# A mixture-of-experts block on one core: the first five expert tiles formed in the last steps of the mixer stage, and the early sums' pieces gathered in each group's first step

## The reference, cut to what matters

```python
h = _layernorm(x) * (1 + ca) + sa
x = x + ga * mixer(h)                    # silu(h @ Win + b), a decaying scan over time, @ Wout
h = _layernorm(x) * (1 + cb) + sb
logits = h @ Wr + br                     # 8 experts, each token goes to its best two
u = layernorm(relu(h @ W1[e] + b1[e]))   # 128 -> 512
y = layernorm(relu(u @ W2[e] + b2[e]))   # 512 -> 128
x = x + gb * (gate0 * y[e0] + gate1 * y[e1])
```

## Time and profile before

| | us |
|---|---|
| median of three runs | 512.86 |
| the profiled execution's own time | 515.06 |
| its span, first to last instruction | 513.1 |
| PE busy | 487.1 (95%) |
| DVE busy | 445.1 (87%) |
| ACT busy | 412.6 (80%) |
| POOL busy | 360.1 (70%) |

### The profile page before, as it was taken

The page is one execution under the profiler, slowest core; times in us unless marked ns, Lnnn a source line. Parts: engine busy times, 40 slices in busy tenths (PEclk is TensorE's granted clock), DMA queues, the critical chain, the costliest instruction groups (busy, mean ns, idle before and its releaser), DMA issues. The chain is left out here.

```text
span 513.1 us, 15015 instructions
## 1 busy us (share of the span) xinstructions
PE 487.1 (95%) x3051; PEld 372.0 (72%) x3051; DVE 445.1 (87%) x2217; ACT 412.6 (80%) x1140; POOL 360.1 (70%) x483
## 2 busy tenths in 40 slices
PE   7989999999987799999999999999999999999994
PEld 6445656555545588888888778888888888888861
DVE  7779999998887599888887789999999999999994
ACT  3679887978764588889888888898888898999984
POOL 1003666666667778888888878788787788988871
PEclk9999999999995699999999999999999999999998
DMA  6980111154111568878726686765766667666665
GB/s 167 309 240 21 46 48 46 48 130 114 52 47 55 135 151 164 161 225 198 178 89 157 178 204 162 191 194 159 208 190 145 192 208 203 175 180 207 189 177 164
DMA packets 80329, 78.36 MB, mean 153 GB/s; under 512 B 11420, under 2 KB 73015, under 8 KB 80242
## 3 DMA queue, kind: packets, MB, share of 16 engines
q1 hardware_dynamic: 71826, 60.48, 46.9%
q0 software_dynamic: 8416, 16.93, 9.3%
HBM read 55.20 MB, written 22.62 MB: 152 GB/s over the span
## 5 line engine op out<-in xcount | busy, mean ns | idle before, releaser
L683 POOL DMA_INDIRECT expert_rows<-rows_ring,slot x128 | 123.3, 964 | 94.5 <-issue 78.4
L711 POOL DMA_INDIRECT expert_results<-y,target x119 | 120.8, 1015 | 30.6 <-issue 24.5
L1725 PE MATMUL bank<-W,h2T 128*128 x720 | 97.4, 278 | 1.8 <-issue 0.8
L1725 PEld LDWEIGHTS bank<-W,h2T 128*128 128x128 f32 x720 | 88.2, 193 | 13.1 <-issue 6.7
L906 ACT ACTIVATE v<-wmod 128x128 f32<-128x128 f32 x135 | 41.8, 310 | 40.0 <-DVE vg L1409 35.0
L1612 PE MATMUL bank<-W1hi,h3hi 128*128 x135 | 66.6, 494 | 1.4 <-DVE h3lo L1176 1.4
L792 ACT ACTIVATE n<-X,nm,rs 128x128 f32<-128x128 f32 x128 | 54.1, 485 | 12.8 <-DVE nm L1343 12.8
L1398 DVE SCALAR_TENSOR_TENSOR wmod<-bank,rse,shifts 128x128 f32<-128x128 f32 x119 | 41.0, 344 | 24.2 <-PE bank L1725 23.3
L1181 DVE BATCH_NORM_STATS2 stf<-h1T 128x6 f32<-128x512 f32 x90 | 59.3, 659 | 0.4 <-ACT h1T L803 0.4
L1620 PE MATMUL bank<-ident_wr,h1T 128*128 128x128 f32 x360 | 55.2, 276 | 0.0
L1613 PE MATMUL bank<-W1lo,h3hi 128*128 x135 | 54.4, 403 | 0.0
(11 more groups left out here) (249 smaller groups left out, 1196.9 us busy)
## 6 DMA issues: line engine op xcount, KB each, us to landing
shifts<-expert_shifts SPq DMA_DIRECT2D x119, 192.0 KB
hrow<-expert_rows SPq DMA_DIRECT2D x135, 65.0 KB
xi<-expert_results SPq DMA_DIRECT2D x12, 512.0 KB, 5.2
out_x<-X SPq DMA_DIRECT2D x15, 256.0 KB
X<-in_L_attn_x SPq DMA_DIRECT2D x7, 512.0 KB, 7.4
b_ring<-b_two_parts SPq DMA_DIRECT2D x135, 4.0 KB
W1lo<-in_L_ffn_W SPq DMA_DIRECT2D x4, 512.0 KB, 6.7
expert_rows<-rows_ring,slot POOLq DMA_INDIRECT x128
```

Of the source, the lines that this page charges most:

```text
L683: nc.gpsimd.indirect_dma_start(out=rows_d, out_offset=bass.IndirectOffsetOnAxis(ap=slot[q][:, n // TOPK, n % TOPK:n % TOPK + 1], axis=0), ...
L711: nc.gpsimd.indirect_dma_start(out=results_d, out_offset=bass.IndirectOffsetOnAxis(ap=target[i % TARGETS][:], axis=0), in_=y[k], in_offset ...
L1725: ins = mm(acc, rT[(s - 4) % DEPTH][:, ch * P:(ch + 1) * P], W2[:, bass.ds(e4 * CF + ch, 1), :], start=(ch == 0), stop=(ch == CF - 1))
```

## The change

**Tiles 0 to 4 in the first stage.** Before, tiles 0 and 1 were turned in mixer step 16 and their hidden products stood at the ends of steps 16 and 17; tile 2 and all later ones had their hidden products in `expert_step(s)`. Now the hidden products of tiles 0 and 1 stand in step 16, those of tiles 2 and 3 in step 17 and those of tile 4 in step 18, with the rounding on ACT and DVE, the turns and the first value products placed between the parts of the mixer and the routing. On DVE the low part of tile 2 now stands between the maximum and the index search of batch 14, and that of tile 4 between those of batch 15; they wait for ACT, which waits for PE's turns. The two last steps of scaling W2 move to the end of step 17. On PE 7 and 9 products of the identity with itself (`keep_busy`, into a bank that nobody reads) stand in step 16, where PE waits. `expert_step` leaves out for tiles up to 4 what was done. The last count of routed tokens goes into another bank.

**Pieces gathered.** `pieces_at(i)` now gives all pieces whose tile lies in the group that begins at i, and nothing for the other steps. On ACT they stand behind the first `hidden_turned` of the group, ahead of the relu, the scale and the root of the step (before: at the end of the step). On DVE the sums stand in the same step (before: in the next). SP's program, `piece_tile` and the places of the loads are as before.

```diff
-        first_rows = [bank[4][:, 0:P], bank[0][:, 0:P]]
+        first_rows = [bank[n][:, 0:P] for n in (4, 5, 5, 4)]
-        EARLY_H = 2
+        EARLY_H = 4
         def pieces_at(i):
-            return [(b, j) for b in range(EARLY) for j in range(J) if piece_tile(b, j) == i]
+            return [(b, j) for b in range(EARLY) for j in range(J) if piece_tile(b, j) // TOGETHER * TOGETHER == i]
...
+                if s == B + 1:
+                    high_part(2, first_rows[2])
+                    hidden(0)
+                    high_part(3, first_rows[3])
...
                 if s == B:
-                    for i in range(EARLY_H):
-                        high_part(i, first_rows[i])
+                    high_part(0, first_rows[0])
+                    high_part(1, first_rows[1])
                 if s == B + 1:
-                    hidden(0)
+                    hidden(1)
+                    hidden_turned(0)
...
             run(mixer_step, FIRST1)
-            hidden(1)
-            hidden_turned(0)
+            high_part(EARLY_H, rows_bank(EARLY_H)[:, 0:P])
+            hidden(2)
+            hidden_turned(1)
+            act.wait_ge(stf_ready, 1)
+            hidden(3)
...
-                if on(s - 3, EXPERT_TILES) and s > 3 and turned_first:
+                if on(s - 3, EXPERT_TILES) and s > 4 and turned_first:
                     hidden_turned(s - 3)
+                for b, j in pieces_at(s):
+                    early_y0g(b, j)
...
-                for b, j in pieces_at(s):
-                    early_y0g(b, j)
...
                 if s == B + 1:
-                    for i in range(EARLY_H):
-                        low_part(i, first_rows[i])
+                    low_part(0, first_rows[0])
+                    low_part(1, first_rows[1])
                 if s == B + 2:
                     hidden_stats(0)
+                    hidden_stats(1)
...
+                if s == B + 1:
+                    low_part(2, first_rows[2])
+                if s == B + 2:
+                    low_part(EARLY_H, rows_bank(EARLY_H)[:, 0:P])
...
+                if s == B + 1:
+                    low_part(3, first_rows[3])
...
+                if s == B + 1:
+                    scale_w2(B + 2, 0)
+                    scale_w2(B + 2, 1)
...
-                for b, j in pieces_at(s - 1):
+                for b, j in pieces_at(s):
                     early_sum(b, j)
...
                     load_expert(0)
+                    keep_busy(7, to=1)
...
+                if s == B + 1:
+                    hidden(2)
+                    load_expert(3)
+                if s == B + 2:
+                    pe.wait_ge(rows_ready, B)
+                    turn_rows(EARLY_H, rows_bank(EARLY_H)[:, 0:P])
+                    pe.wait_ge(w2_ready, W2_STEPS)
+                    values(0)
+                    hidden(EARLY_H)
+                    load_expert(EARLY_H + 1)
...
                 if s == B:
-                    for i in range(EARLY_H):
-                        turn_rows(i, first_rows[i])
+                    turn_rows(0, first_rows[0])
+                    pe.wait_ge(x1_ready, B)
+                    turn_rows(1, first_rows[1])
+                    keep_busy(9, to=1)
+                if s == B + 1:
+                    pe.wait_ge(h3lo_ready, EARLY_H)
+                    turn_hidden(0)
...
-                if s in (B, B + 1):
-                    hidden(s - B)
-                    load_expert(s - B + 1)
+                if s == B:
+                    hidden(0)
+                    load_expert(1)
+                    hidden(1)
+                    load_expert(2)
+                    turn_rows(2, first_rows[2])
+                    turn_rows(3, first_rows[3])
                 if s == B + 1:
-                    turn_hidden(0)
+                    hidden(3)
+                    load_expert(EARLY_H)
+                    turn_hidden(1)
...
+            pe.wait_ge(placed_ready, B)
             pe.wait_ge(carry_ready, B)
-            pe.wait_ge(x1_ready, B)
-            mm(bank[5][:, 0:E], ones[:], hots[B % 2][:, J, :], start=True, stop=True).then_inc(count_done, 1)
+            mm(bank[7][:, COUNTS], ones[:], hots[B % 2][:, J, :], start=True, stop=True).then_inc(count_done, 1)
+            turn_hidden(EARLY_H - 2)
+            pe.wait_ge(counts_ready, 1)
+            turn_rows(EARLY_H + 1, rows_bank(EARLY_H + 1)[:, 0:P])
...
-                if on(s, EXPERT_TILES) and s >= EARLY_H:
+                if on(s, EXPERT_TILES) and s > EARLY_H:
                     hidden(s)
```

More of the change, by code:

```diff
@@ L892, in expert_step @@
                 last_of_group = s % TOGETHER == 0
-                if on(s + 1, EXPERT_TILES) and s + 1 >= EARLY_H:
+                if on(s + 1, EXPERT_TILES) and s + 1 > EARLY_H:
                     high_part(s + 1, rows_bank(s + 1)[:, 0:P])
@@ L906, in expert_step @@
                     nc.scalar.activation(v[1 - q][:], v0[1 - q], ACT.Relu).then_inc(v_ready, 1)
-                if on(s - 3, EXPERT_TILES) and s > 3 and not turned_first:
+                if on(s - 3, EXPERT_TILES) and s > 4 and not turned_first:
                     hidden_turned(s - 3)
@@ L1076, in round2_table @@
                     dve.wait_ge(count_done, 1)
-                    vec.tensor_copy(cnt_i[:, GROUPS - 1, :], bank[5][:, 0:E]).then_inc(counts_ready, 1)
+                    vec.tensor_copy(cnt_i[:, GROUPS - 1, :], bank[7][:, COUNTS]).then_inc(counts_ready, 1)
                 if n == 1:
@@ L1216, in mixer_step @@
                                       ALU.add).then_inc(logit_ready, 1)
-                scale_w2(s, 0)
+                if s < B + 2:
+                    scale_w2(s, 0)
                 round1_table(s, 0)
@@ L1224, in mixer_step @@
                     ins.then_inc(best_ready, 1)
-                scale_w2(s, 1)
+                if s == B + 1:
+                    low_part(2, first_rows[2])
+                if s == B + 2:
+                    low_part(EARLY_H, rows_bank(EARLY_H)[:, 0:P])
+                if s < B + 2:
+                    scale_w2(s, 1)
                 round1_table(s, 1)
@@ L1249, in mixer_step @@
                     vec.tensor_copy(rows[k3][:, :, 1], besti[p][:, :, 0]).then_inc(ids_ready, 1)
+                if s == B + 1:
+                    low_part(3, first_rows[3])
+                if s == B + 2:
+                    dve.wait_ge(best_ready, B)
+                    vec.tensor_tensor(lead[:], best[:, :, 0], best[:, :, 1], ALU.subtract).then_inc(lead_ready, 1)
                 if on(a, B):
@@ L1372, in _ @@
             run(mixer_step, 1)
-            dve.wait_ge(best_ready, B)
-            vec.tensor_tensor(lead[:], best[:, :, 0], best[:, :, 1], ALU.subtract).then_inc(lead_ready, 1)
             dve.wait_ge(table_ready, 1)
@@ L1468, in expert_step @@
                     ins = hidden_norm(s, q, p)
-                if on(s - 2, EXPERT_TILES) and s > 2 and not stats_first:
+                if on(s - 2, EXPERT_TILES) and s > 3 and not stats_first:
                     hidden_stats(s - 2)
@@ L1507, in _ @@
             run_tiles(expert_step)
-            for i in range(EXPERT_TILES - 1, EXPERT_TILES + 2):
+            for i in range(EXPERT_TILES, EXPERT_TILES + 2):
                 for b, j in pieces_at(i):
@@ L1621, in turn_hidden, with values @@
                 ins.then_inc(tr_done, 1)
+            def values(i):
+                e = expert_of[i]
+                acc = value_bank[:, 0:D].rearrange("p (o d) -> p o d", o=1)
+                pe.wait_ge(rT_ready, i + 1)
+                if i > 0:
+                    pe.wait_ge(v0_ready, i)
+                for ch in range(CF):
+                    ins = mm(acc, rT[i % DEPTH][:, ch * P:(ch + 1) * P], W2[:, bass.ds(e * CF + ch, 1), :],
+                             start=(ch == 0), stop=(ch == CF - 1))
+                ins.then_inc(y_done, 1)
             def mixer_step(s, q, e, k):
@@ L1705, in expert_step @@
+            turn_hidden(EARLY_H - 2)
+            pe.wait_ge(counts_ready, 1)
+            turn_rows(EARLY_H + 1, rows_bank(EARLY_H + 1)[:, 0:P])
             def expert_step(s, n):
-                q = n % 2
-                if on(s, EXPERT_TILES) and s >= EARLY_H:
+                if on(s, EXPERT_TILES) and s > EARLY_H:
                     hidden(s)
-                if on(s + 2, EXPERT_TILES):
-                    if s % TOGETHER == 0 and s > 0:
+                if on(s + 2, EXPERT_TILES) and s >= EARLY_H:
+                    if s % TOGETHER == 0:
@@ L1711, in expert_step @@
                         pe.wait_ge(r_ready, s)
                     turn_rows(s + 2, rows_bank(s + 2)[:, 0:P])
-                if on(s + 1, EXPERT_TILES) and s + 1 > EARLY_H:
+                if on(s + 1, EXPERT_TILES) and s > EARLY_H:
                     load_expert(s + 1)
[L1715 to L1719, removed]
+                if on(s - 4, EXPERT_TILES) and s > EARLY_H:
+                    if s == TABLE2_STEPS:
@@ L1727, in expert_step @@
-                    ins.then_inc(y_done, 1)
```

(3 more changed lines are left out.)

10 lines of the change are left out of this document (1 added, 9 removed).

## The result

| | before | after |
|---|---|---|
| median of 6 runs each, same chip | 513.14 us (512.39 to 513.94) | 538.03 us (536.94 to 539.25) |
| ratio, 95% interval | | 1.0459 [1.0433, 1.0485] |
| span of the profiled execution | 513.1 us | 537.1 us |
| first hidden product of tile 5 / 48 / 80 / 108 | 178.83 / 279.72 / 356.98 / 424.20 | 170.98 / 280.66 / 356.84 / 448.26 |

The change makes the kernel slower by 24.9 us; I had forecast 531.6, 18.7 over the median, and a range of 519 to 539. The last row of the table tells the story. PE is 7.9 us ahead at tile 5, has nothing left of it at tile 48, is level with before at tile 80, and loses 24.2 us between tiles 80 and 108.

What follows compares the result with a forecast made beforehand. POOL's full list, through SP, was taken to hold PE from 163.5 to 301 us, PE itself to bound tiles 80 to 108; 0.6 - 2.4 + 4.6 + 10.6 + 0.4 + 4.9 = +18.7 on 512.86 gave 531.6 us, range 519 to 539.

Steps and rivals of the forecast that it cites:

- lead of the first part on the path, POOL's delay: End of first stage: PE's 7 us lead is worth nothing on the path; added DVE waits delay POOL's list, +0.6 us.
- sums no longer in odd steps, tiles 80 to 108: Tiles 80 to 108: sums in odd steps delay DVE; gathering them gives back 2.4 us (0 to 2.9).
- batch 0's piece: Step 52 instead of 53: the piece waits for its load and delays tile 54, +0.4 us (0 to 1.5).
- four waits for loads, clock held: Steps 80, 88, 96, 104: pieces of batches 4 to 7 wait for SP's loads, +4.6 and +10.6 us.
- fall of the clock in them: PE's clock drops to its lower level in two of the four load waits, +4.9 us (0 to 10).
- The bound: Up to tile 48: POOL's full list holds SP, and SP holds PE, turning tile 48's rows no earlier than 274.88.
- Rival (d): POOL's list isn't full, the 7 us lead passes: 524.6 with waits (chance 0.05), 504.5 without (0.03).
- The landing: Time from SP's issue of a load until it lands, taken as 4.2 us, lower end 3, upper 5.2.
- Rival (b): Clock falls in all four waits and at the first stage's end, POOL starting 3 us late: 539 us, chance 0.10.
- The identity products: End of first stage: 16 added products, some 0.11 us each, lie in PE's waits and cost nothing.
- The shared port: DVE and GpSimd exclude each other there; two sums in a row could be held, shrinking the 2.4 us to nothing.
- Rival (c): SP issues batch 4's load before about 353, so loads are in time: 511.5 us, faster, chance 0.09.

Runs made afterwards that it cites:

- e6: The changed kernel with 13 identity products on PE in each of the four waits for late loads: 531.86 us, 1.0346.
- e5: e3 with POOL's row stores thinned to one in every fourth tile up to tile 24: 507.28 us, 0.9876.
- e9: e5 with the pieces of batch 0 left in their own tiles: 507.89 us, 0.9889.
- e10: e1 with POOL's row stores thinned to one in every fourth tile up to tile 24: 507.46 us, 0.9886.
- e3: The changed kernel with SP's loads of batches 4 to 10 moved to the first tile of their group: 512.60 us, 0.9954.
- e1: The changed kernel with the gathered pieces put back, so the first part of the change alone: 513.04 us, 0.9971.
- e11: The changed kernel with SP's loads of batches 4 to 7 one place sooner in SP's list: 518.02 us, 1.0089.
- e12: e1 without its 16 identity products at the end of the first stage: 517.27 us, 1.0084.

## Why the prediction was right, and which terms were off

| term | forecast | found |
|---|---|---|
| lead of the first part on the path, POOL's delay | +0.6 | tile 48 +0.94, tile 60 -0.06: 0 |
| sums no longer in odd steps, tiles 80 to 108 | -2.4 | -2.7, with the four late groups at 9.19 |
| batch 0's piece | +0.4 | within the first row |
| four waits for loads, clock held | +15.2 | +19.1 (e6) |
| fall of the clock in them | +4.9 | +7.8 by the traces, 6.2 by the medians |
| sum | +18.7 | +24.2; the spans differ by 24.0 |

The path was right, and the size only because the range had room: 538.03 is 1 us from the upper end of 519 to 539, and outside the 527.5 to 537 to which I gave 0.50.

**The bound** was right in every step: POOL at 267, SP's shifts behind it, PE's wait of 4.14 us in step 45 (I said 3 to 5), tile 48's rows at 275.7 (I said 274.9; the clock fell in that wait, which I had not counted). Rival (d), that POOL's list isn't full, is out: the lead passes only where that list is thinned, in e5, e9 and e10.

**The landing was the term that was mis-sized most.** I took 4.2 us for the load, from batch 0's single piece, which gave an upper end for one load; the page's median over twelve, 5.2, stood beside it. The four took 5.06, 5.38, 6.04 and 5.06 in the changed kernel and 4.82, 6.50, 5.13 and 4.96 in e6, where the mean is 5.35: 1.15 over mine, four times, is 4.6, and the waits were off by 3.9. The rest of that sum holds: without the fall of the clock tile 82 comes at 366.07 in e6, where I had 365.8, and each group of e6 loses ACT's wait less 0.1 to 0.4 us. Two slips in my sum come to 0.5 us and change nothing: 3.5 three times is 10.5, and 6.5 us at 3.51 for 2.30 lose 2.2.

**The clock** fell with all four waits and not with two. The Trainium skill, TensorE: Matmul & The Clock Gate, section "HAM oscillation — how this bites in real kernels", has a burst behind each wait for a load begin at the lower level; here single waits of 3.3 to 5.2 us on PE did it each time, and the stretches behind them stood at 0.51 to 0.57. Behind the shortest it was still up when PE began again: 1.00 from 439.7 to 441.0, where the eight value products take 1.15 us, and low only after that; there the measurement differs from the Trainium skill. Rival (b) had this half. That 538 lies next to its 539 is in part luck: of what I was short by, the clock is 2.9 us and the landing 3.9, and (b)'s other half, the low clock that starts POOL 3 us late, did not come (1.00 from 154.5 to 167.5, a wait of 0.57 us).

**The identity products** I costed at nothing since they lie in PE's waits, and the delay of POOL at 0.6 as "nearer to a clock that holds". These are one term: the products are what holds the clock there. Without them POOL's wait is 3.3 us, near the upper end of my bound (3), so the choice between the ends was right, but its reason was not named.

**The sums** hardly hold DVE up in the changed kernel: the longest takes 0.553 us instead of 0.986:

```profile
L1514 DVE SCALAR_TENSOR_TENSOR n<-xi,gate,n x44: 339/344/553, 293.1 to 521.0; 128x128 f32<-128x128 f32 x44
```

The shared port of the Trainium skill, SBUF — State Buffer, section "🔬 SBUF: two separate sides", by which sums in a row might both have been held up, did not take the 2.7 back here. In e5 the trace agrees with it as far as it goes: the longest sum takes 1.172 us, and two pairs take 1.64 each. The 2.7 itself leans on the 9.19. In e3, where no load is late, the seven groups take 2.1 us less than before (65.16), and e1, which gathers nothing, has 0.6 of that (66.65).

**Rival (c)** gave its own test, a load before about 353. e11 issues it at 352.39 and 0.54 us of wait are left; e3 issues it at 347.67, none is left, and the time is 512.6 where (c) had 511.5.

## What to carry to other kernels

When work is gathered into an earlier step, move what feeds it by as much, and find the feeder's place in its own queue: here two to five microseconds on SP lay between two neighbouring places in the list. A lead made in front of a full queue is worth little until that queue is thinned, and thinning it without the lead is worth little too; the two belong in one change (e10: 507.46 us against 513.37). For a transfer that something will wait for, take the median of all its kind, not the one that happened to be consumed early.

## What was not expected of the hardware

An identity product of 128x128 f32 is two records on PE and costs 0.23 us (13 of them in 3.06 us), twice what I took. In e6 three microseconds of them inside a wait of over four kept the granted clock at 1.00 although PE then stood idle for another 1.00 us; the same wait unfilled dropped it to 0.54. And PE's clock reached the queue of another engine: at the end of the first stage POOL's wait for DVE is 0.77 us with the 16 identity products (e1, clock 1.00) and 3.34 us without (e12, 0.61).
